# One broadcast multiply in place of four per-head multiplies: scaling gathered rows in the last attention layer of a four-layer graph network

## The reference

```
Wh = einsum('ni,hio->hno', h, W)                  # 4 heads x 32 features for each node
e  = leaky_relu(e_l[:, src] + e_r[:, dst]) + log(clip(edge_weight))
alpha = exp(e.T - segment_max(e.T, dst)[dst])     # one weight for each edge and head
alpha = alpha / (segment_sum(alpha, dst)[dst] + 1e-8)
out = segment_sum(alpha[:, :, None] * Wh[src], dst) + bias
x = x + out
```

## Time and profile before

| | |
|---|---|
| median of 3 runs | 7494.23 us (7484.67 to 7494.71) |
| the profiled execution | 7494.23 us |
| its span, first to last instruction | 7492.3 us |
| the last layer's gathers | 5350.3 to 7340.2 us of the span |
| VectorE busy over the span | 4567.3 us, 61% |
| GpSimd busy over the span | 1843.6 us, 25% |
| TensorE busy over the span | 5794.6 us, 77% |

### The profile page before, as it was taken

One profiled execution on the slowest core, in us unless ns is written; L12 is line 12 of the kernel. 1 busy time (PEld: TensorE's weight loads), 2 busy tenths in 40 slices (PEclk: granted clock), 3 DMA queues, 4 the chain that ended last, 5 costly groups with the idle time before them and its releaser, 6 DMA issues.

```text
span 7492.3 us, 170747 instructions
## 1 busy us (share of the span) xinstructions
PE 5794.6 (77%) x48472; PEld 4913.8 (66%) x48472; DVE 4567.3 (61%) x15387; ACT 2412.8 (32%) x7276; POOL 1843.6 (25%) x1782
## 2 busy tenths in 40 slices
PE   1777777777777779999999999998256656666665
PEld 1555555555555559999999999998244444444444
DVE  6999999999999982222111111112178878877876
ACT  2666666666666651111110000002022222222222
POOL 2000000000000000000000000000777777777771
PEclk9998988989889899999999999999577877777786
DMA  6766766667667677666677666674222222222221
GB/s 186 288 274 278 284 278 281 280 275 287 276 272 286 277 296 273 261 262 266 278 280 278 276 276 276 278 280 164 47 59 60 59 61 59 60 61 59 59 60 29
DMA packets 261054, 1542.95 MB, mean 206 GB/s; under 512 B 56235, under 2 KB 86965, under 8 KB 233836
## 3 DMA queue, kind: packets, MB, share of 16 engines
q1 hardware_dynamic: 201380, 1406.77, 47.9%
q0 software_dynamic: 59008, 129.85, 7.2%
q10 hardware_dynamic: 130, 0.80, 0.0%
HBM read 795.75 MB, written 743.08 MB: 205 GB/s over the span
## 4 chain that ended last, share of the span: by engine, by line
PE 44%; DVE 18%; POOL 17%; issue 13%; ACTq 3%; ACT 3%; DMA 2%; DVEq 0%; SPq 0%; POOLq 0%
PE psum L1118 29%; POOL field L810 16%; DVE field L1549 12%; PE psum L1083 8%; ACT field L923 2%; ACTq L908 2%; PE psum L1307 2%; PE psum L1285 1%; DVE field L1542 1%; DVE field L1543 1%; PE psum L1184 1%; DVE field L1544 1%; ACTq L923 1%; DMA field<-in_edge_attr 1%; PE psum L1054 0%
## 5 line engine op out<-in xcount | busy, mean ns | idle before, releaser
L1118 PE MATMUL psum<-field 128*128 128x128 f32 x19208 | 2255.2, 277 | 25.8 <-issue 18.4
L1118 PEld LDWEIGHTS psum<-field 128*128 128x128 f32 x19208 | 2232.4, 189 | 26.2 <-issue 18.6
L1083 PE MATMUL psum<-field 128*128 128x200 bf16 (+1 forms) x14112 | 1924.9, 281 | 133.1 <-DVE field L1549 115.4
L923 ACT COPY field<-psum x4704 | 1657.9, 416 | 959.0 <-PE psum L1083 664.4
L1549 DVE TENSOR_TENSOR field<-field 128x1176 bf16<-128x1176 bf16 x2352 | 1648.9, 761 | 0.0
L810 POOL DMA_INDIRECT field<-head_table,cmp x1563 | 1513.7, 968 | 476.6 <-issue 474.1
L1083 PEld LDWEIGHTS psum<-field 128*128 128x128 bf16 x14112 | 1077.1, 101 | 426.3 <-issue 159.4
L1074 PE MATMUL psum<-zero_b 128*128 128x2 bf16 x4704 | 807.3, 172 | 455.8 <-ACT field L923 447.4
L1898 DVE TENSOR_SCALAR field<-field,work 128x33 f32<-128x33 f32 x6252 | 968.7, 260 | 2.8 <-ACT work L994 2.0
L1074 PEld LDWEIGHTS psum<-zero_b 128*128 128x128 bf16 x4704 | 478.6, 102 | 642.9 <-issue 577.9
L1014 ACT COPY field<-psum x1611 | 433.7, 269 | 1125.7 <-PE psum L1307 813.8
(11 more groups left out here) (289 smaller groups left out, 2688.0 us busy)
## 6 DMA issues: line engine op xcount, KB each, us to landing
adj<-field SPq DMA_DIRECT2D x882, 800.0 KB, 5.1
field<-adj SPq DMA_DIRECT2D x196, 3200.0 KB, 10.0
field<-head_table,cmp POOLq DMA_INDIRECT x1563
field<-in_edge_attr SPq DMA_DIRECT2D x4, 3072.0 KB, 28.6
head_table<-field SPq DMA_DIRECT2D x7, 476.0 KB, 3.2
tile_rows<-field SPq DMA_DIRECT2D x1, 3328.0 KB, 20.9
right_edges<-zeros SPq DMA_DIRECT2D x1, 3328.0 KB, 19.9
place_rows<-right_edges SPq DMA_DIRECT2D x25, 128.0 KB, 2.8
```

What stands on the lines that cost most here:

```text
L923: act.copy(evac[:, :, bass.ds(place, SEG)], build_banks[:, bass.ds(bank, NSEG * SEG)].rearrange("p (w c) -> p w c", w=NSEG)).then_inc(pair ...
L1083: mm = pe.matmul(build_banks[:, bass.ds(cur[j % ROUND], end - first)], hot, pr[:, first:end], start=False, stop=True, skip_group_check=True)
L1118: mm = pe.matmul(ps_y[slot][:, 0:D], source[:, hi, :], adj_in[slot][:, :, 2 * hi:2 * hi + 2], start=(hi == 0), stop=(hi == NB - 1))
```

## The change

In `steps_of`, four `tensor_scalar` instructions for each tile, one for each head (33 columns, with the weight as a per-partition scalar read from `alpha`), become one `scalar_tensor_tensor` over all four heads (4 x 33 columns). Its second tensor is the tile's four weights, each repeated over its head's 33 columns by a step of zero. The values that are written are the same, (row x 1.0) x weight. Semaphores, group size and order stay.

```
                 for t in range(0, steps, SUB):
                     if t < tiles:
                         for u in range(t, min(t + SUB, tiles)):
-                            for h in range(HEADS3):
-                                r = rows[:, i * WIN + u, h, 0:DH3 + 1]
-                                ins = dve.tensor_scalar(r, r, alpha[:, h, u:u + 1], None, ALU.mult)
+                            r = rows[:, i * WIN + u, :, 0:DH3 + 1]
+                            al = alpha[:, :, u].rearrange("p (h a) -> p h a", a=1).to_broadcast([P, HEADS3, DH3 + 1])
+                            ins = dve.scalar_tensor_tensor(out=r, in0=r, scalar=1.0, in1=al, op0=ALU.mult, op1=ALU.mult)
                         ins.then_inc(rows_scaled, 1)
```

## The result

The changed kernel takes 7597.1 us (median of 4 runs, 7585.0 to 7602.0) against 7494.5 us before: 1.0139 times as long, with a 95% interval of 1.0119 to 1.0158. That is 103 us slower, where 2 us was forecast and 7516 us was the end of the range. One of the four runs of before took 9084 us, as runs on the two chips described further down do, and is left out of the ratio; the other three have a median of 7494.2 us.

A forecast was written before the change was run, and what follows sets the result against it. GpSimd's stream of gathers was taken to bound the kernel. 7494.2 us, + 11 for holds on gathers, - 2.8 for the old multiplies, - 6.1 at the end, gave 7496.3, taken as 7496 us; range 7482 to 7516.

The forecast's parts named there:

- The pacer: Last layer: GpSimd's gathers, 1.27 us a tile, set the time; VectorE's 570 us saved would be nearly all hidden.
- The new instruction: VectorE's multiply: 132 columns take 296 ns, 0.22 us a tile in a burst; a burst falls from 4.78 to 1.84 us.
- What a faster VectorE does next: VectorE waits for `row_added`, no later group late; TensorE starts windows 3 us earlier, its last-gather wait rising to about 7 us.
- The end: Behind window 23's last landing, two first bursts on the chain shrink by 3.2 and 2.9 us: -6.1 us.
- The old multiplies: Gathers beside the old multiplies' bursts lose 0.004 us each in the mean; 2.8 us in all fall away.
- The hold on the gathers: In new bursts, a gather is held at one point until the running instruction's columns end: 0.043 us each, +11 us.
- the row I relied on: A gather at 5352.82 beside softmax scans running until 5353.56 took 0.22 us more, not 0.62: held for one instruction.
- The bounds: Limits on the hold: nothing if short instructions slip by, +28 us if it covers the whole 0.22 us.
- Rival A: The new instruction holds up everything a gather does, 0.29 us a gather, +75 us: 7560 us; chance 0.08.

The follow-up runs named there:

- psum: Changed kernel with the weights read from the PSUM bank instead of their SBUF copy, so one SBUF input instead of two: 7479.8 us, 0.9983 of before.
- tt: Changed kernel with tensor_tensor (row x weight) in place of scalar_tensor_tensor: 7586.1 us, 1.0132 of before.
- best: Changed kernel with four 264-column instructions a group, weights read from PSUM, and ScalarE's copy of them to SBUF dropped: 7469.1 us, 0.9978 of before.
- heads: Changed kernel with four 33-column instructions a tile, 32 back to back in a group: 7478.6 us where gathers pace the windows, 9141 us first on another chip.
- fence1: Changed kernel with VectorE waiting on its own completion after each new instruction but the last of a group: 7489.3 us, 0.9997 of before.
- fence4: Changed kernel with VectorE waiting on its own completion only after the fourth of a group's eight instructions: 7518.5 us, 1.0037 of before.
- long: Changed kernel with four back-to-back instructions a group, one for each head over its 8 tiles, 264 columns each: 7592.4 us, 1.0137 of before.
- half: Changed kernel with the new instruction on partitions 0 to 63 alone, same columns, part of the work left out: 8981 us where gathers have slack.
- between: Changed kernel with a one-column memset between two of the new instructions and no wait: 7484.2 us, 0.9997 of before, where gathers pace the windows.
- scan: Changed kernel with each product replaced by a 136-column scan on 128 partitions, eight back to back, values wrong: 9143 us where gathers have slack.
- heads_c: The kernel of heads run again where the gathers pace the windows: 7478.6 us, 0.9994 of before.
- heads_b: The kernel of heads run again on another chip, where gathers have slack: 9143 us, 0.995 of before there.

## Why the prediction was wrong

**The pacer: right.** The gathers pace the last layer before and after, without idle time above 0.31 us. VectorE's busy time fell by 603 us (4567.3 to 3964.2; 570 forecast), which bought nothing.

**The new instruction: right.** It takes 285 ns and 0.206 us from start to start, where 296 ns and 0.22 us were worked out; a burst takes 1.73 us, not 1.84. The repeated operand makes no instruction longer than was worked out.

**What a faster VectorE does next: right but for one wait.** The new waits for `row_added` made no group late; TensorE's wait for the first burst fell by 3.2 us a window (2.9 forecast). TensorE's wait for the last gather is 11.7 us, not about 7: each of the 24 windows of gathers became 105.3 / 24 = 4.4 us longer, which follows from the hold.

**The end: right, in a stretch that varies by as much.** -6.1 us was forecast. The chain of the change has the first burst of window 24 at 1.75 us where it was 4.78, and with window 23's at the same length the two save 6.3 us:
```profile
7485.24 1.75 DVE field L1898 x8
```
The whole stretch behind the stream of gathers is 178.2 us in the change and in psum against 186.0 before. But it is 185.7 in tt, whose bursts are as short: there TensorE's groups behind the two bursts (from the first seam product to L1846, then to L1930) take 61.9 and 64.5 us against 58.2 and 60.8 in the change. So the whole stretch alone, of one execution each, doesn't show the 6 us; the bursts on the chain do.

**The old multiplies: not refuted.** 2.8 us were to fall away; psum, which holds nothing in their place, has 1509.9 us of gathers against 1513.7, 3.8 less. Kernels without holds differ by more than that (best 1503.9, heads 1511.5), so one profile of each can't show so small a term.

**The hold on the gathers: wrong, and the step is this sentence: "it is held for the rest of the instruction that is then running, not of the burst".** It was +11 us in the sum and is about +110 (107.5 more gather time and 3.8 that the old multiplies gave back). For products that stand alone the term had the right size: fence1, where each waits for the one before, has 1517.4 - 1509.9 = 7.5 us of it. What failed was the carrying over. The evidence was of two kinds in the earlier trace rows: products of which the second stands 0.03 us behind the end of the first, with a wait between them, and scans back to back. Neither is a product back to back with its like. The change, fence4, long and half show that such a run of 132 or 264 columns each can hold to its end; between shows that one instruction of another kind in each gap removes the holds; scan and half together show that the row I relied on doesn't carry over to these products.

**The bounds: wrong with it.** The bound of +28 us still assumed a hold that ends with the instruction. A hold to the end of the burst, 184 x 1.4 x 0.87 = 224 us at most with the forecast's counts, was put aside on the scans' evidence and should have stood as a rival with a chance of its own. About half of it came, since the 184 x 1.4 = 258 gathers were in fact 130 that were held (of 193 with their point in a burst), while the 0.87 us for each was right (0.88). The mean gather of 1.037 us is outside the 0.95 to 0.99 us that the prediction gave as its sign of being wrong. Its chance of 0.81 was stated for 7480 to 7509 us and its range as 7482 to 7516; 7597 lies outside both.

**Rival A** gave 7560 us, nearer to the result than the forecast, for the wrong reason: the median gather didn't change. The Trainium skill (SBUF — State Buffer, SBUF: two separate sides) has the rule that a VectorE instruction with two SBUF inputs takes the shared pair against a GpSimd operation that reads SBUF. The runs agree: in psum, where one input lies in PSUM, nothing is held to the end of a burst (longest gather 1.44 us), and with both in SBUF gathers last up to 2.71 us. The same section has the pair held for the whole instruction; that alone is too little for runs of products, as 2.31 us beside a 0.285 us instruction shows.

## What to carry to other kernels

Where GpSimd's own DMA issue paces a stage, judge a VectorE change by what it does to GpSimd first and by VectorE's time last: here 603 us less of VectorE's work came with +103 us of time. Back-to-back products of 132 or more columns with both inputs in SBUF are the form to avoid beside such a stream; here one operand left in PSUM, a different instruction between each two or a wait after each removed the cost. A bound for an unseen operation must be read from rows of the same kind in the same arrangement (same operation, no wait between); where there are none, the worse arrangement belongs in the range.

## What the runs showed of the hardware that was not expected

- Eight two-input products of 132 columns back to back, 0.206 us apart, held two thirds of the gathers whose point lay in them (130 of 193) to the end of the eighth: single ones last up to 2.71 us against 0.95.
- 32 of 33 columns, 0.104 us apart, in a run of some 3.5 us, held none of 508 to the end in heads_c, but one for 2.78 us in heads_b; eight scans of 136 columns in 2.76 us held none for longer than 0.22 us.
- Four products of 264 columns with both inputs in SBUF, 1.45 us in all, cost as much as eight of 132 (7592 and 7597 us).
- A memset of one column between two products, with no wait, ended these holds, and the products then start 0.22 us apart in place of 0.206.
